# An encoder block with two mixture-of-experts layers on one core: more steps between the stages of the experts loop, attention values kept in SBUF, router product moved behind the first projection

## The reference, cut to what matters

```python
x = x + 0.5 * ffn(layernorm(x))     # mixture of experts, 8 experts, top 2
x = x + attn(layernorm(x))          # 16 heads of width 16, causal, latent projections
x = x + 0.5 * ffn(layernorm(x))

def ffn(x):
    logits = x @ gate_weight.T                      # (N, 8)
    top_w, top_i = top_k(softmax(logits), 2)        # normalised; rerouted by similarity
    gu = einsum('nh,efh->enf', x, gate_up_proj); g, u = split(gu, 2)
    y = einsum('enf,ehf->enh', silu(g) * u, down_proj)
    return einsum('ne,enh->nh', combine, y)

def attn(x):
    Q, K, V = (x@W_dq)@W_uq, (x@W_dkv)@W_uk, (x@W_dkv)@W_uv
    return softmax_causal(Q K^T / 4) V @ W_o
```

## Time and profile before

| | us |
|---|---|
| median of 3 runs (lowest, highest) | 1361.29 (1356.99, 1362.87) |
| profiled execution, whole | 1358.71 |
| its span, first to last instruction | 1356.9 |

### The profile page before, as it was taken

One profiled execution on the slowest core, in us unless ns is written; L12 is line 12 of the kernel. 1 busy time (PEld: TensorE's weight loads), 2 busy tenths in 40 slices (PEclk: granted clock), 3 DMA queues, 4 the chain that ended last, 5 costly groups with the idle time before them and its releaser, 6 DMA issues. The chain is left out here.

```text
span 1356.9 us, 27575 instructions
## 1 busy us (share of the span) xinstructions
PE 1104.6 (81%) x7114; PEld 667.6 (49%) x7117; DVE 853.9 (63%) x2534; ACT 678.2 (50%) x1676; POOL 462.5 (34%) x528
## 2 busy tenths in 40 slices
PE   3538999993885599999999999999869279999960
PEld 2236888772332134344344444444347168878750
DVE  4773444334883788888888788888147744443327
ACT  3513544441564057666666566667636225544430
POOL 3536777671343400000000000000027457777650
PEclk9857999996787589999999999999989659999985
DMA  7701222225656914445545534540046202222239
GB/s 230 223 0 63 94 94 94 94 90 192 209 188 168 168 15 65 67 69 77 74 64 71 76 67 61 81 65 10 10 150 224 78 26 96 93 94 96 85 111 331
DMA packets 130286, 141.06 MB, mean 104 GB/s; under 512 B 46800, under 2 KB 104592, under 8 KB 130192
## 3 DMA queue, kind: packets, MB, share of 16 engines
q1 hardware_dynamic: 112144, 98.04, 32.7%
q0 software_dynamic: 13824, 37.77, 8.2%
q10 hardware_dynamic: 4224, 4.19, 0.9%
HBM read 86.88 MB, written 52.69 MB: 103 GB/s over the span
## 5 line engine op out<-in xcount | busy, mean ns | idle before, releaser
L1410 ACT ACTIVATE t_prob<-t_psS 128x512 f32<-128x512 f32 (+3 forms) x768 | 327.2, 495 | 185.2 <-PE t_psS L1342 150.2
L1430 DVE CUSTOM_DVE_ANT_0 t_psR<-t_psR,all_causal 128x128 f32<-128x128 f32 (+3 forms) x512 | 247.1, 503 | 62.9 <-PE t_psR L1320 53.8
L1320 PE MATMUL t_psR<-stacks_kst,stacks_qst 96*128 96x512 bf16 (+3 forms) x768 | 234.9, 346 | 33.3 <-PEq L888 20.1
L1339 PE MATMUL t_psS<-stacks_qst,stacks_kst 99*128 99x512 bf16 (+3 forms) x768 | 223.7, 332 | 2.4 <-ACT t_prob L1410 1.5
L1434 DVE TENSOR_REDUCE t_maxp<-t_psR 128x1 f32<-128x512 f32 x256 | 175.7, 686 | 21.1 <-PE t_psR L1320 20.8
L1320 PEld LDWEIGHTS t_psR<-stacks_kst,stacks_qst 96*128 96x128 bf16 x768 | 70.1, 98 | 214.3 <-DVE t_maxp L1430 112.4
L1353 PE MATMUL t_psO<-t_prob,t_vst 128*32 128x512 f32 (+3 forms) x1536 | 163.6, 498 | 3.0 <-ACT t_prob L1410 1.1
L1311 POOL COPY t_vst<-stacks_v_rows 128x512 f32<-128x512 f32 x16 | 9.8, 614 | 439.2 <-DMA stacks_v_rows<-v_rows 439.0
L678 PE MATMUL ae_psG<-a_w,ae_xT 128*128 x432 | 116.3, 405 | 3.1 <-DVE ae_xT L765 2.4
L678 PE MATMUL be_psG<-b_w,be_xT 128*128 x432 | 115.7, 403 | 3.0 <-DVE be_xT L765 2.3
L1342 PE MATMUL t_psS<-all_causal_t,all_ident_bf 128*128 128x128 bf16 x512 | 109.6, 221 | 0.0
(11 more groups left out here) (289 smaller groups left out, 1899.2 us busy)
## 6 DMA issues: line engine op xcount, KB each, us to landing
qk_parts<-q_parts SPq DMA_DIRECT2D x32, 384.0 KB, 2.6
stacks_qst<-qk_parts SPq DMA_DIRECT2D x96, 128.0 KB, 4.6
stacks_kst<-qk_parts SPq DMA_DIRECT2D x96, 128.0 KB, 7.4
q_yk<-y_rows SPq DMA_DIRECT2D x16, 512.0 KB, 6.3
s_yk<-y_rows SPq DMA_DIRECT2D x16, 512.0 KB, 10.0
o_rows<-t_orow SPq DMA_DIRECT2D x32, 136.0 KB, 8.8
bl_raw<-o_rows SPq DMA_DIRECT2D x8, 544.0 KB, 4.0
xn_rows<-al_xn SPq DMA_DIRECT2D x8, 512.0 KB, 3.8
```

Of the source, the lines that this page charges most:

```text
L1320: nc.tensor.matmul(psR[bank][:, 0:w], qst[slot][0:KROWS, h, i * P:(i + 1) * P], kst[slot][0:KROWS, h, k0:k0 + w], start=True, stop=True).t ...
L1339: ins = nc.tensor.matmul(ps, kst[k][0:MROWS, h, j * P:(j + 1) * P], qst[k][0:MROWS, h, a:(c + 1) * 512], start=True, stop=a > j * P)
L1410: nc.scalar.activation(prob[j % 2][:, h, a:(c + 1) * 512], psS[n % ST_BANKS][:, a - c * 512:512], ACT.Exp, scale=DK ** -0.5).then_inc(exp_ ...
L1430: ins = nc.vector.tensor_tensor_reduce(psR[bank][:, 0:w], psR[bank][:, 0:w], T.causal[:, 512 - w:512], 1.0, -BIG, ALU.add, ALU.max, maxp[: ...
```

## The change

- Experts: x is transposed 3 steps ahead (was 2), h 2 steps behind its gate_up (was 1), down runs 4 steps behind (was 2). xT, hT and hid get rings of 4. The scatter of tile t-12 follows the gather of tile t (was t-8). Three rounds of POOL's loop over 8 tiles are written out (were two), and the closing part has 12 scatters (was 8).
- Values: V stays in SBUF in `A.values`; the DRAM tensor v_rows, its 8 stores and 16 loads, the waits for the stores and the staging tiles vx and v_rows are gone. POOL's copy to vst reads A.values.
- Logits: `scores` stands behind the first `project` of its step, `turn_scores` at s = 2 (was 1); on ACT the copy to lT stands at the start of s = 1 (was ahead of s = 0), the copy to logits at s = 3 (was 1).

```diff
@@ phase_logits, PE and ACT @@
             def step(c, b, has):
-                if has(-2):
-                    scores(c - 2)
                 for s in range(U):
                     if attended and has(0):
                         project(c, s)
+                    if has(-2) and s == 0:
+                        scores(c - 2)
...
-                    if has(-2) and s == 1:
+                    if has(-2) and s == 2:
                         turn_scores(c - 2)
...
-                if has(-2):
-                    act.wait_ge(l_done, c * 2 - 3)
-                    nc.scalar.copy(lT[:], psL[0][:, 0:P]).then_inc(l_copied, 1)
                 for s in range(U):
+                    if has(-2) and s == 1:
+                        act.wait_ge(l_done, c * 2 - 3)
+                        nc.scalar.copy(lT[:], psL[0][:, 0:P]).then_inc(l_copied, 1)
@@ phase_experts @@
         RING = 4
+        X_AHEAD, H_BEHIND, Y_BEHIND = 3, 2, 4
+        BLOCKS = UT // RING
+        STORE_BLOCKS = 3
-        xT = [M.sb(f"xT{part}", [P, 2, DC, P], F32R) for part in range(2)]
-        hT = [M.sb(f"hT{part}", [P, 2, DC, P], F32R) for part in range(2)]
+        xT = [M.sb(f"xT{part}", [P, RING, DC, P], F32R) for part in range(2)]
+        hT = [M.sb(f"hT{part}", [P, RING, DC, P], F32R) for part in range(2)]
-        hid = M.sb("hid", [P, 2, F])
+        hid = M.sb("hid", [P, RING, F])
...
+            def copies(it, s):
+                first, second = 2 * it + s // RING + 1, 2 * it + s // RING + 1 - STORE_BLOCKS
+                return first + (max(second, 0) if isinstance(it, int) else second)
...
-                hold(pool, index_ready, UT // RING + (it - 1) * (2 * UT // RING) + 2 * (s // RING) + 2 if not first else s // RING + 1, T)
+                hold(pool, index_ready, copies(it, s), T)
...
             def scatter(it, s):
-                i = s % RING
-                hold(pool, y_ready, it * UT + s + 1, T)
+                i, col = s % RING, (s + STORE_BLOCKS * RING) % UT
+                hold(pool, y_ready, it * UT + (s + 1 - STORE_BLOCKS * RING), T)
...
-                    if not isinstance(it, int) or it > 0:
-                        scatter(it - 1, s)
-            body(0)
-            body(1)
-            with pool.Fori(2, ITS) as it:
+                    if some(it * UT + (s - STORE_BLOCKS * RING)):
+                        scatter(it, s)
+            for it in range(3):
                 body(it)
+            with pool.Fori(3, ITS) as it:
+                body(it)
...
-                    if some(t - 1):
-                        transpose_h(t - 1, s + 1)
-                    if some(t + 2):
-                        transpose_x(it + (s + 2) // UT, (s + 2) % UT)
-                    if some(t - 2):
-                        down(t - 2, s, expert(before if s < 2 else now, s - 2))
+                    if some(t - H_BEHIND):
+                        transpose_h(t - H_BEHIND, s - H_BEHIND)
+                    if some(t + X_AHEAD):
+                        transpose_x(it + (s + X_AHEAD) // UT, (s + X_AHEAD) % UT)
+                    if some(t - Y_BEHIND):
+                        down(t - Y_BEHIND, s - Y_BEHIND, expert(before if s < Y_BEHIND else now, s - Y_BEHIND))
@@ Stacks, phase_qkv, phase_attention @@
-    N_LOADS = len(Q_PARTS) + len(K_PARTS) + 1
+    N_LOADS = len(Q_PARTS) + len(K_PARTS)
+        self.values = M.sb("values", [P, NT, D])
-        self.v_rows = [M.sb(f"v_rows{s}", [P, QT, HG * DK]) for s in range(SLOTS)]
...
-        src = self.v_dram[bass.ds(b * S, S), bass.ds(hg * (HG * DK), HG * DK)]
-        sp.dma_start(self.v_rows[slot][:], src.rearrange("(j p) w -> p j w", p=P)).then_inc(self.loaded[slot], 16)
...
-                hold(sp, v_ready, c * 2 + 2, T)
-                sp.dma_start(v_view[:, bass.ds(c * U, U), :], vx[:, b]).then_inc(v_stored[b], 16)
...
-            for b in range(2):
-                sp.wait_ge(v_stored[b], 16 * (CH // 2))
...
-                wait(act, v_stored[b], (c // 2) * 16)
-                nc.scalar.copy(vx[:, b, 2 * i:2 * i + 2, :], psV[i][:].rearrange("p (s d) -> p s d", s=2)).then_inc(v_ready, 1)
+                nc.scalar.copy(A.values[:, bass.ds(c * U + 2 * i, 2), :], psV[i][:].rearrange("p (s d) -> p s d", s=2)).then_inc(v_ready, 1)
...
-                nc.gpsimd.tensor_copy(heads(vst[k], VW)[:, :, 0:DK], heads(v_rows[k], DK)).then_inc(pool_done, 1)
+                rows = A.values[:, bass.ds(b * QT, QT), bass.ds(hg * (HG * DK), HG * DK)]
+                nc.gpsimd.tensor_copy(vst[k][:].rearrange("p j (h w) -> p j h w", w=VW)[:, :, :, 0:DK],
+                                      rows.rearrange("p j (h w) -> p j h w", w=DK)).then_inc(pool_done, 1)
```

More of the change, by code:

```diff
@@ L353, in step @@
                         nc.scalar.copy(xT[:, :, s, :], psT[s % 2][:, 0:D].rearrange("p (k t) -> p k t", k=DC)).then_inc(xT_ready, 1)
-                    if has(-2) and s == 1:
+                    if has(-2) and s == 3:
                         act.wait_ge(l_done, c * 2 - 2)
@@ L641, in body @@
                     gather(it, s)
-                    if not isinstance(it, int) or it > 0:
-                        scatter(it - 1, s)
-            body(0)
-            body(1)
-            with pool.Fori(2, ITS) as it:
+                    if some(it * UT + (s - STORE_BLOCKS * RING)):
+                        scatter(it, s)
+            for it in range(3):
                 body(it)
-            for s in range(UT):
+            with pool.Fori(3, ITS) as it:
+                body(it)
+            for s in range(STORE_BLOCKS * RING):
+                it = ITS + s // UT
                 if s % RING == 0:
-                    places(ITS, s)
-                    pool.wait_ge(index_ready, UT // RING + (ITS - 1) * (2 * UT // RING) + s // RING + 1)
-                scatter(ITS - 1, s)
+                    places(it, s % UT)
+                    pool.wait_ge(index_ready, copies(ITS - 1, UT - RING) + s // RING + 1)
+                scatter(it, s % UT)
             for i in range(RING):
@@ L707, in body @@
                         before = word(it - 1)
[L708 to L715 removed]
+                    if some(t - H_BEHIND):
[4 more added lines that the diff above has]
+                        down(t - Y_BEHIND, s - Y_BEHIND, expert(before if s < Y_BEHIND else now, s - Y_BEHIND))
+            for s in range(X_AHEAD):
                 transpose_x(0, s)
             steps(body, pe)
[L718 removed]
             last = word(ITS - 1)
[L720 to L721 removed]
+            for t in range(MT, MT + Y_BEHIND):
+                if t - H_BEHIND < MT:
+                    transpose_h(t - H_BEHIND, t - H_BEHIND)
+                down(t - Y_BEHIND, t - Y_BEHIND, expert(last, t - Y_BEHIND))
         @block.scalar
@@ L746, in body @@
                     nc.scalar.activation(sg[:, s % 2, :], psG[s % 2][:, 0:F], ACT.Silu).then_inc(sg_ready, 1)
-                    if some(t - 1):
-                        high_h(t - 1, s + 1)
-                    if some(t + 2):
-                        high_x(t + 2, s)
-                    if some(t - 2):
-                        copy_y(it - (s < 2), (s - 2) % UT)
-            for s in range(2):
+                    if some(t - H_BEHIND):
+                        high_h(t - H_BEHIND, s - H_BEHIND)
+                    if some(t + X_AHEAD):
+                        high_x(t + X_AHEAD, s + X_AHEAD)
+                    if some(t - Y_BEHIND):
+                        copy_y(it - (s < Y_BEHIND), (s - Y_BEHIND) % UT)
+            for s in range(X_AHEAD):
                 high_x(s, s)
             steps(body, act)
-            high_h(MT - 1, MT - 1)
-            for s in (UT - 2, UT - 1):
-                copy_y(ITS - 1, s)
+            for t in range(MT, MT + Y_BEHIND):
+                if t - H_BEHIND < MT:
+                    high_h(t - H_BEHIND, t - H_BEHIND)
+                copy_y(ITS - 1, (t - Y_BEHIND) % UT)
         @block.vector
@@ L774, in body @@
                     dve.wait_ge(sg_ready, t + 1)
-                    wait(dve, ht_done, t - 1)
-                    nc.vector.tensor_tensor(hid[:, s % 2, :], sg[:, s % 2, :], psG[s % 2][:, F:2 * F], ALU.mult).then_inc(hid_ready, 1)
-                    if some(t - 1):
-                        low_h(t - 1, s + 1)
-                    if some(t + 2):
-                        low_x(t + 2, s)
-            for s in range(2):
+                    wait(dve, ht_done, t + 1 - RING)
+                    nc.vector.tensor_tensor(hid[:, s % RING, :], sg[:, s % 2, :], psG[s % 2][:, F:2 * F], ALU.mult).then_inc(hid_ready, 1)
+                    if some(t - H_BEHIND):
+                        low_h(t - H_BEHIND, s - H_BEHIND)
+                    if some(t + X_AHEAD):
+                        low_x(t + X_AHEAD, s + X_AHEAD)
+            for s in range(X_AHEAD):
                 low_x(s, s)
             steps(body, dve)
-            low_h(MT - 1, MT - 1)
+            for t in range(MT - H_BEHIND, MT):
+                low_h(t, t)
 def phase_sum(nc, T, tag, R, x, y_dram, out):
@@ L1603, in program @@
```

(1 more changed line is left out.)

45 lines of the change are left out of this document (19 added, 26 removed).

## The result

The changed kernel took 1351.35 us (median of 20 runs, 1346.16 to 1356.67) against 1360.2 for the kernel before in 20 runs on the same chips: ratio 0.9942, 95% interval 0.9924 to 0.9959 (the quotient of the two medians is 0.9935). Predicted was 1355.4 / 1361.29 = 0.9957. The way was right, and the size short by 2 us by the first measurement and 5 us by the second. The two differ because the 20 runs of the changed kernel fall into two groups, 11 from 1346.16 to 1351.62 and 9 from 1353.97 to 1356.67, while all six of the second measurement lie between 1347.30 and 1350.89.

A forecast was written before the change was run, and what follows sets the result against it. The limit was taken to change by stage: POOL in experts, DMA backlog before attention, xn and DVE's normalisation in logits. Values -5.1 and experts -0.8 took 1358.71 to 1352.8 us profiled, 1355.4 in the median; range 1349 to 1361.5.

The forecast's parts named there:

- What bounds the kernel: By stage: POOL in experts, DMA backlog before attention, the wait for xn in second logits, DVE's normalisation in first logits.
- Values, -5.1: Between projections and attention: two V stores at 1.4 us each and one load at 2.3 leave the DMA backlog, -5.1 us.
- Rival C: Between projections and attention: the last q/k store's landing sets the end, so only the wait goes; 1359.5 us, chance 0.17.
- the 2.3 from the stretch at 100 GB/s: Before attention: the V load in 256-byte pieces priced at 2.3 us from a profile stretch carrying mostly such a load.
- The sum of -3.6: Before attention: alternative values total, -3.6 us, with the load at 0.8 us by the skill's 341 GB/s for 1 MB.
- Experts, -0.8: Two experts stages: POOL stays the limit, the last scatter starts slightly earlier with the odd gap kept; -0.4 us each.
- Rival E: POOL's expert loop: register work for a two-term wait adds 0.6 us to each loop block; 1369.8 us, chance 0.08.
- 0.88 against 0.27: Experts: POOL's time in us between last index copy and gather, in the loop against written out; cited for the slower rival.
- Rival B: Second logits: PE was the limit, so 4.2 us more goes; 1351.2 us, chance 0.12.
- Logits: Both logits stages: 0 us; in the second, PE's wait for xT goes but xn is late next, bounds -4.2 to +5.1.
- rival D: First logits: one stretched normalisation less or more, 3.8 us; 1351.6 or 1359.2 us, chance 0.06 below, 0.07 above.
- What I counted at exactly nothing: All stages the change doesn't touch: taken as unchanged, 0 us.

The follow-up runs named there:

- the second measurement: The changed kernel run again unchanged, with the runs of the experiments: 1350.24 us, ratio 0.9918 to the kernel before.
- flat_after: The changed kernel with all nine rounds of POOL's expert loop written out instead of three: 1339.33 us, ratio 0.9837 to the kernel before.
- stores_kept: The changed kernel with the eight V stores to DRAM and their waits back, nobody reading them: ratio 0.9941 to the kernel before.
- loads_kept: The changed kernel with loads of the V loads' shape back, into a tile nobody reads, no V stores: ratio 0.9960 to the kernel before.
- third_body: The kernel before with only a third round of POOL's expert loop written out: 1356.52 us, ratio 0.9973 to the kernel before.

## Why the prediction came out as it did

**What bounds the kernel** held as far as it was tested. Least sure was POOL in the experts: flat_after changes POOL's instructions alone, and the stages shorten by it. Between projections and attention the engines' idle stretch and the full DMA engines are there again, but what fills SP's queue was read wrongly (below). That a normalisation beside W.low paces the first logits was not tested by a run of its own.

**Values, -5.1**: too large, and wrong in its parts. From the last cT copy to attention it is 22.0 to 22.3 us in three traces without V transfers that have POOL's loop (20.2 to 21.8 in four with it written out), against 25.5: -3.4 in the mean, -4.1 in the pair. The steps that failed are the prices: stores 2 x 1.4 measured 0.7 together when alone, the load 2.3 measured 1.7. The remaining 1.0 appears only when stores and load are both there, which a sum over bytes can't see; it is hardly more than the traces scatter. Rival C (-1 in all) is refuted by the size, but the sentence against it, that a full queue is bytes, is wrong: two V stores in the queue leave the issue of the last four at 2.61 us, one small load makes it 8.16. Part of the gain may be lost again behind the transition, which the prediction left out: from PE's first attention product to the first copy of oT it is 58.1 to 59.6 us (mean 58.6) in the five traces with V transfers, 58.8 with the load alone, and 59.2 to 59.8 (mean 59.6) in the eight without V loads. The ranges overlap, and why it should be so no run shows. The load's price lies nearer to the 2.3 from the stretch at 100 GB/s than to the 0.8 us estimated from the Trainium skill's 1 MB row (DMA: Bandwidth & Descriptors, section Bandwidth). The sum of -3.6 with that row lies near the -3.4 measured, but by luck, since its stores stand at 2.8.

**Experts, -0.8**: too small, by the one stall that I carried over unchanged. In four stage pairs with the new rings and the loop (the changed kernel twice, stores_kept, loads_kept) the two stages sum to 403.3 to 403.8; before to 406.1: -2.6. The gap is 1.94 in each, -3.9. Against that stands +1.3, where I had -0.8 (gap kept): above all the waits in the last scatters, which I had counted as gone for 0.8 a stage. They are 1.35 above the usual 0.30 in the first stage and 0.55 in the other, where the kernel before had 0.9 in each. "Occurs once" was in the row; that it stood at the same DMA in both layers I had not looked up, and that would have spoken for the order of the instructions as its cause, and so for something that the change touches. Why it is there stays open. The new rings and distances themselves gained little: 406.1 to 404.4 us goes by the third written-out round (third_body), 403.3 to 403.8 are reached with them, and with the loop written out they gain nothing.

**Rival E**: wrong in its direction. The sum of two register terms cost 0.02 us in a block. What it rested on, 0.88 against 0.27, was real, and the larger chance was to take the 0.6 away.

**Rival B** named 1351.2, next to the 1351.35 measured, but what it said didn't happen: the second logits didn't become 4.2 us shorter but 1.0 longer. That its number was met is chance. The chances as a whole leaned the other way: 0.51 on no change to speak of and 0.41 on more than 0.5% faster, and 0.6 to 0.8% were measured.

**Logits**: the mechanism in the second layer was right. PE's first projection comes earlier and then waits for xn. Its size, 0, was +1.0 (110.5, 110.4, 110.4, 109.9, 110.4, 110.5 with the new place against 109.2 to 109.6 in eight traces with the old), within the bounds: 0.1 a step in the loop, 0.5 behind it. In the first layer 95.3 to 96.1 in seven traces with the new place, 97.1 to 98.1 in six with the old and 95.8 in a seventh: -1.6, rival D by halves. The price of one stretched normalisation is not a fixed 3.8: it takes 1.99 to 5.47 us in these traces. Of its four instructions one takes 0.40 us alone and 1.9 beside one of POOL's, and the number that is hit differs from trace to trace. Together -0.6.

**What I counted at exactly nothing** moved most: -4.5 in the projections, +3.1 in attention. In all traces the seven projection steps take 80.0 to 80.7 us (eight traces), 84.7 to 84.8 (two) or 86.6 to 87.4 (four). Five traces with V transfers have 84.8, 80.7, 87.1, 80.5 and 80.0, the unchanged kernel twice among them: the transfers don't decide it. But the changed kernel had 80.3 and 80.6, and stores_kept and loads_kept, which differ from it little, 80.7 and 80.2, while all four with the written-out loop had 84.7 or more. So the good case may belong to when a program reaches this stage, and not be pure chance; that stays open. The parts above (-3.4, -2.6, -0.6, and -0.2 in the final stage, the sum) come to -6.8 us, or -5.9 if the 0.9 at the start of attention is real; the medians moved by 8.9 and 9.8. Projections that fall more often into the good case would fill that difference, but this was not shown. The two groups of the changed kernel's runs lie about as far apart as the good and the bad case; its two traces are both of the lower group and both in the good case, and no run of the upper group was traced. That the forecast of -5.9 came near is in part luck: the values were counted 1.7 too high at least, the experts 1.8 too low.

## What to carry to other kernels

Look up a stall that nothing released at its count in every stage of its kind; if it recurs at the same count, as here in ten stages of ten, it goes with the program, and an edit of the order may take it away. Where the engine that issues indirect DMAs bounds a stage, compare its blocks inside and outside a register loop before adding buffers: here 0.6 us a block was worth more than the rings. A small load in short pieces ahead of the last stores can cost more than its bytes: here 256 KB took 1.7 us, where 378 GB/s would make it 0.7, and the stores behind it took 8.2 us to issue instead of 2.6. And one trace of each kernel can mislead: the largest difference of the pair, 4.5 us in the projections, came again, as 4.1, between two traces of the unchanged kernel.

## What was not expected of the hardware

- TensorE's granted clock alternated from step to step in the projections (1.00, 0.68, 0.97 in the three steps shown; 1.00 is 2.4 GHz, 0.50 is 1.2 GHz), though every step has the same products. The first step had the high level in eight traces (7.8 us) and the low one in six (13.3 to 13.8 us). Of seven steps three or four are slow by that, and this is the difference between 80 and 85 to 87 us.
- On one chip the experts stages took 233 to 240 us instead of 200 to 204 with the same code. Each DMA took the same (mean 0.98), but gaps of 1.0 to 3.1 us stood before 15 to 24 of the 144 (before at most 5 elsewhere), and "remote" is given as the releaser of some. Everything outside the experts took what it took elsewhere.
- Four stores of 384 KB were issued in 2.3 to 2.8 us without, and 6.8 to 8.5 us with, one load of 1,024 pieces of 256 bytes ahead of them.
